# Last stage of a mixture-of-experts block: VectorE adds both partial sums of every group, and the weights are transposed and copied ahead

## The chip, the cores and the metric

The kernel runs on one core of a Trainium2 chip. The metric is the device time of one execution in microseconds (us). Engines are TensorE (PE), VectorE (DVE), ScalarE (ACT), GpSimd (POOL) and SyncE (SP), which issues most of the DMAs. They work side by side and wait for one another on semaphores.

## The reference

4096 tokens of 256 features pass through a gated recurrent layer and then a mixture-of-experts layer; each adds a layer-normed result to its input. What matters here is the end of the second one:

```python
    gate_up = jnp.einsum('th,ehd->etd', x, gate_up_proj) + gate_up_proj_bias[:, None, :]
    ...
    out = jnp.einsum('etd,edh->eth', (up + 1.0) * glu, down_proj) + down_proj_bias[:, None, :]
    out = out * router_scores.T[:, :, None]
    out = out.sum(axis=0)
    ...
x = x + _layernorm(_L0_ffn_ref(_layernorm(x, axis=-1), ...), axis=-1)
```

Each token has four experts with a score. So its output is the sum of four expert products, each times its score, plus the scores (16 of them, 12 zero) times the biases `down_proj_bias`, then layer-normed and added to the token's input.

## The kernel before

**The stages ahead.** A recurrent stage works on eight blocks of 512 tokens and routes every token's row to its experts' regions in HBM. Then 143 tiles of 128 routed rows go through their expert; GpSimd scatters each tile's result with an accumulating indirect DMA into one of two arrays in HBM, `sums0` and `sums1`, in turn (L1050). The two arrays together hold each token's expert sum.

**The last stage** adds it all up, in eight groups of 512 tokens (`NBLK` groups, `BT` = 4 rows of tokens per partition in each):

- SyncE waits for all scatters, then issues two loads a group, `sums0` into `z[g]` and `sums1` into `z2[g]` (L490, L491), of 512 KB each. Semaphores `blk_in[g]` and `z2_in[g]` tell when they have landed.
- TensorE transposes a group's weights `Wd` (`transpose_weights`, L728; four transposes into one of two PSUM banks, so group g waits for the copy of group g - 2), ScalarE copies them to `sT[g]` in SBUF (`evac_weights`, L965), and TensorE multiplies them with the biases (`biases`, L735; into one of three PSUM buffers, so group g waits until the total of group g - 3 has read its own).
- VectorE makes the total of a group (`total`, L1460): both sums, times a scale `y_inv`, plus the bias product. Groups 0 to 3 (`g < PAIRED`) take two adds on VectorE (L1466, L1468). For groups 4 to 7 GpSimd adds the two sums first (`both`, L1055, with the add at L1058), into `z2[g]`, and VectorE does one add (L1472).
- VectorE takes statistics of each total (L1482). Groups are normalised in three batches, `BATCHES = ((0, 1, 2, 3), (4, 5, 6), (7,))`: after a batch's last group VectorE aggregates (L1485), and computes the scale `r4` and shift `mr4` with a chain of ten small instructions (L1487, `newton` at L1077 to L1084, L1491). `rz_ready` says so.
- ScalarE normalises a group in place (`norm_z`, L982, instruction L987), four instructions a group, and for the last group only shifts the input rows (`shift_last`, L974, instruction L979), which VectorE then adds to the scaled total (`add_last`, L1500).
- GpSimd stores groups 0 to 6 with DMAs that add to the rows already in `out` (L1066); SyncE stores group 7 in two halves (L495).

The order on each engine is written out by hand. TensorE begins with the transposes of groups 0 and 1, and then has the bias of a group and the transposes of the group two further on in turn. ScalarE copies four groups' weights, then, for each of seven groups, copies the weights of the group four further on (while there are any) and normalises the group. GpSimd has its four adds ahead of all stores.

Of the kernel before, what the change touches and what calls it, by code (L numbers as in the profile page):

```python
# [27 lines left out]
NBLK = TOKENS // BLK  # L28
# [29 lines left out]
ROOT_A, ROOT_B = 0.375 * 0.703952253, 0.375 * 0.703952253 * 2.38924456  # L58
SUMS = 2
BATCHES = ((0, 1, 2, 3), (4, 5, 6), (7,))  # L60
PAIRED = 4
PART = 1024
PARTS_GU, PARTS_DN = E * KT * 2 * FF // PART, E * KT * DIM // PART
PARTS = PARTS_GU + PARTS_DN
# [67 lines left out]
def build(nc, x, w_in, w_gate, b_gate, rms_w, w_out, w_router, b_router, w_gu, b_gu, w_dn, b_dn,  # L132
# [3 lines left out]
    ALU = mybir.AluOpType  # L136
# [5 lines left out]
    with ctx:  # L142
# [3 lines left out]
        def sem(name):  # L146
            return ctx.enter_context(nc.semaphore(name))
# [143 lines left out]
        blk_in = [sem(f"blk_in{b}") for b in range(NBLK)]  # L291
# [30 lines left out]
        zero_ready, zero_sent, x1_sent = sem("zero_ready"), sem("zero_sent"), sem("x1_sent")  # L322
        sT_mm, sT_ready = sem("sT_mm"), sem("sT_ready")
        bias_mm, t_ready, rz_ready, yz_ready = sem("bias_mm"), sem("t_ready"), sem("rz_ready"), sem("yz_ready")
        out_sent, both_ready = sem("out_sent"), sem("both_ready")
        shift_ready, last_ready, last_sent = sem("shift_ready"), sem("last_ready"), sem("last_sent")

        block = ctx.enter_context(nc.Block())
# [173 lines left out]
        def _(pe):  # L502
# [225 lines left out]
            def transpose_weights(g):  # L728
                if g >= 2:
                    pe.wait_ge(sT_ready, g - 1)  # L730
                for u in range(BT):
                    last = nc.tensor.transpose(PS[0:E, 6 + g % 2, u * P:(u + 1) * P], Wd[:, BT * g + u, :], ident)
                last.then_inc(sT_mm, 1)
# [9 lines left out]

            pe.wait_ge(y2_ready, TILES + 2)
            pe.wait_ge(s_bdn, 16)
            transpose_weights(0)
            transpose_weights(1)
            for g in range(NBLK):
                biases(g)
                if g + 2 < NBLK:  # L750
                    transpose_weights(g + 2)


        @block.scalar
        def _(act):
# [209 lines left out]
            def evac_weights(g):  # L965
                act.wait_ge(sT_mm, g + 1)
                copy(sT[g], PS[0:E, 6 + g % 2, :]).then_inc(sT_ready, 1)
# [20 lines left out]
                                                bias=mr4[n][:, m + u:m + u + 1], scale=r4[n][:, m + u:m + u + 1])  # L988
                last.then_inc(yz_ready, 1)

            for g in range(4):
                evac_weights(g)
            for g in range(NBLK - 1):
                if g + 4 < NBLK:
                    evac_weights(g + 4)
                norm_z(g)
            shift_last(NBLK - 1)

# [1 line left out]
        @block.gpsimd  # L1000
        def _(pool):
            def wait(s, n):
                pool.wait_ge(s, n)
                if not isinstance(n, int):
                    pool.nop(nofuse=True)

            def scatter(t):

                b = t % 2
                per = BT * TOPK // 2  # L1010
                pool.wait_ge(slot_ready, t + 1)
                pool.wait_ge(lo_ready, t + 1)
                for jk in range(BT * TOPK if t < NBLK - 2 else AHEAD):
                    lane = jk % 2
                    if t or jk >= 2:
                        pool.wait_ge(rows_sent[lane], 16 * (per * t + jk // 2))
                    idx = slot[b][:, jk:jk + 1].bitcast(u32)
                    pool.indirect_dma_start(routed, bass.IndirectOffsetOnAxis(ap=idx, axis=0),  # L1018
                                            rows[b][:, jk // TOPK, :], None).then_inc(rows_sent[lane], 16)

            pool.wait_ge(nrow_out, 16)
            for e in range(E):
                if e % 2 == 0:
                    pool.wait_ge(s_moe[e // 2], 16)
                    pool.wait_ge(squared, 2 + PARTS_DN + e + 1)
                pool.dma_start(W[:, (GU0 + 1 + e) * PART:(GU0 + 2 + e) * PART].rearrange("p (k x) -> p k x", k=KT),  # L1026
                               neg_mem[e:e + 1, :].unsqueeze(1).to_broadcast([P, KT, 2 * FF]),
                               accum_op=ALU.add).then_inc(minus_done, 16)

            for t in range(NBLK - 1):  # L1030
                scatter(t)

            def late_row(n):
                t, jk = divmod(BT * TOPK * (NBLK - 2) + AHEAD + n, BT * TOPK)
                if jk == 0:
                    pool.wait_ge(slot_ready, t + 1)
                    pool.wait_ge(lo_ready, t + 1)
                idx = slot[t % 2][:, jk:jk + 1].bitcast(u32)
                pool.indirect_dma_start(routed, bass.IndirectOffsetOnAxis(ap=idx, axis=0),
                                        rows[t % 2][:, jk // TOPK, :], None).then_inc(rows_sent[jk % 2], 16)  # L1040

            for j in range(TILES):
                u = j % YU
                pool.wait_ge(meta_in[j % MU], 16 * (j // MU + 1))
                if j == 0:
                    pool.wait_ge(zero_sent, 16 * SUMS)
                pool.wait_ge(y2_ready, j + 3)
                if j >= SUMS:
                    pool.wait_ge(y_sent[(j - SUMS) % YU], 16 * ((j - SUMS) // YU + 1))
                pool.indirect_dma_start(sums[j % SUMS], bass.IndirectOffsetOnAxis(ap=dst[j % MU], axis=0),  # L1050
                                        yb[u], None, compute_op=ALU.add).then_inc(y_sent[u], 16)
                if j % 2 and j // 2 < 2 * BT * TOPK - AHEAD:
                    late_row(j // 2)

            def both(g):  # L1055
                pool.wait_ge(blk_in[g], 32)
                pool.wait_ge(z2_in[g], 16)
                nc.gpsimd.tensor_tensor(z2[g].rearrange("p u d -> p (u d)"), z[g].rearrange("p u d -> p (u d)"),  # L1058
                                        z2[g].rearrange("p u d -> p (u d)"), ALU.add).then_inc(both_ready, 1)

            for g in range(PAIRED, NBLK):
                both(g)
            pool.wait_ge(x1_sent, 16 * (NBLK - 1))
            for g in range(NBLK - 1):
                pool.wait_ge(yz_ready, g + 1)
                pool.dma_start(out_v[:, BT * g:BT * (g + 1), :], z[g], accum_op=ALU.add).then_inc(out_sent, 16)  # L1066
# [3 lines left out]
        def _(dve):  # L1070
# [389 lines left out]
            def total(g):  # L1460
                flat, flat2 = [a[g].rearrange("p u d -> p (u d)") for a in (z, z2)]
                bias = PS[:, 2 * (g % 3):2 * (g % 3) + 2, :].rearrange("p b x -> p (b x)")
                if g < PAIRED:
                    dve.wait_ge(blk_in[g], 32)
                    dve.wait_ge(bias_mm, g + 1)
                    L(v.scalar_tensor_tensor(flat, flat, y_inv, bias, ALU.mult, ALU.add))  # L1466
                    dve.wait_ge(z2_in[g], 16)
                    v.scalar_tensor_tensor(flat, flat2, y_inv, flat, ALU.mult, ALU.add).then_inc(t_ready, 1)  # L1468
                else:
                    dve.wait_ge(bias_mm, g + 1)  # L1470
                    dve.wait_ge(both_ready, g + 1 - PAIRED)
                    v.scalar_tensor_tensor(flat, flat2, y_inv, bias, ALU.mult, ALU.add).then_inc(t_ready, 1)  # L1472

            def batch(b):

# [74 lines left out]
```

## Time and profile before

| | |
|---|---|
| times of three runs | 746.56, 746.67, 748.28 us; median 746.67 |
| profiled execution | 747.17 us, of which 745.4 us are the span that the trace shows |
| busy over the span | PE 632.9, DVE 517.5, ACT 458.0, POOL 403.3 us |
| chain that ended last, by engine | PE 66%, DVE 10%, ACT 9%, DMA 8% |

The profile's busy times are sums over the whole span. The last stage, from about 682 us on, is 8% of it, and another set of engines works in it than in the stages ahead. So it is read from views of that stretch alone: the busy time by window, the waits, the chain of work that ended last, and the instructions in order of time. In those rows "W" is the SBUF array in which `z`, `z2` and `sT` lie, "small" holds the statistics and scales, "PS" is PSUM, "X" holds input rows. An idle time in brackets stands ahead of the first instruction of its row, with what ended it. "W<-W,small,PS 128x1024" is an instruction on 128 partitions of 1024 numbers each.

### The profile page before, as it was taken

How to read it: one execution, taken by the hardware profiler on the slowest of the kernel's cores; microseconds unless marked ns; L12 is line 12 of the kernel's file. 1: busy time of each engine (PE TensorE's matmuls, PEld its weight loads, DVE VectorE, ACT ScalarE, POOL GpSimd, SP SyncE). 2: the span in 40 equal slices, each digit the busy share in tenths (PEclk: the TensorE clock that was granted, in tenths of full speed). 3: DMA queues.
4: the chain of work that ended last, by engine and by line, in shares of the span. 5: the costliest groups of instructions: out<-in, count | busy, mean ns of one | idle time of the engine just before them, and what ended most of it. 6: DMA issues, size and time to landing. Idle time of an engine off the chain costs nothing.

```text
span 745.4 us, 13253 instructions
## 1 busy us (share of the span) xinstructions
PE 632.9 (85%) x3666; PEld 408.4 (55%) x3666; DVE 517.5 (69%) x1468; ACT 458.0 (61%) x929; POOL 403.3 (54%) x302
## 2 busy tenths in 40 slices
PE   6988979888998954598999999999999999985460
PEld 2454646555564643455666666666666666653240
DVE  3737687876788786877777777777777777751964
ACT  3689787546656525365776677677667766750054
POOL 0012213447677646546777887666666666663342
PEclk9999989796999965599999999999999999995555
DMA  7979999653233224256888877777776776646967
GB/s 234 419 304 156 275 237 293 185 171 124 88 117 121 99 90 139 95 102 111 188 170 164 131 132 118 113 114 115 116 114 106 117 108 101 100 57 144 342 99 127
DMA packets 110694, 114.32 MB, mean 153 GB/s; under 512 B 31426, under 2 KB 100306, under 8 KB 108962
## 3 DMA queue, kind: packets, MB, share of 16 engines
q0 software_dynamic: 34784, 49.70, 38.9%
q1 hardware_dynamic: 75842, 63.79, 28.7%
q8 instruction: 34, 0.56, 0.3%
q14 instruction: 34, 0.28, 0.1%
HBM read 54.94 MB, written 58.51 MB: 152 GB/s over the span
## 4 chain that ended last, share of the span: by engine, by line
PE 66%; DVE 10%; ACT 9%; DMA 8%; issue 3%; POOL 1%; SPq 0%; ACTq 0%; DVEq 0%; POOLq 0%
PE PS L683 8%; PE PS L684 8%; PE PS L685 8%; PE PS L531 7%; DMA routed<-arena,small 6%; PE PS L672 4%; PE PS L703 4%; PE PS L704 4%; PE PS L691 4%; PE PS L705 4%; PE PS L566 3%; PE PS L558 2%; DMA sums<-arena 1%; PE PS L541 1%; ACT arena L777 1%
## 5 line engine op out<-in xcount | busy, mean ns | idle before, releaser
L1050 POOL DMA_INDIRECT sums<-arena x143 | 223.2, 1561 | 107.5 <-ACT arena L757 42.9
L1018 POOL DMA_INDIRECT routed<-arena,small x104 | 117.7, 1132 | 77.7 <-DMA routed<-arena,small 52.7
L1446 DVE TENSOR_SCALAR arena<-PS,small 128x256 f32<-128x256 f32 x143 | 77.7, 543 | 90.0 <-ACT arena L960 89.9
L531 PE MATMUL PS<-arena 128*128 128x512 f32 x256 | 130.9, 656 | 7.5 <-ACT arena L757 7.4
L960 ACT ACTIVATE arena<-PS,small 128x256 f32<-128x256 f32 x143 | 67.7, 473 | 104.7 <-PE PS L685 104.7
L757 ACT ACTIVATE arena<-PS 128x512 f16<-128x512 f16 (+1 forms) x179 | 104.5, 590 | 26.5 <-PE PS L574 10.9
L683 PE MATMUL PS<-W,arena 128*128 x286 | 109.6, 383 | 0.2 <-DVE arena L1448 0.2
L684 PE MATMUL PS<-W,arena 128*128 x286 | 109.5, 383 | 0.0
L685 PE MATMUL PS<-W,arena 128*128 x286 | 109.5, 383 | 0.0
L531 PEld LDWEIGHTS PS<-arena 128*128 128x128 f32 x256 | 51.7, 213 | 64.7 <-issue 60.8
L703 PE MATMUL PS<-W,arena 128*128 x286 | 78.1, 273 | 4.8 <-DVE arena L1436 4.7
L704 PE MATMUL PS<-W,arena 128*128 x286 | 78.1, 273 | 0.0
L705 PE MATMUL PS<-W,arena 128*128 x286 | 78.0, 273 | 0.0
L777 ACT ACTIVATE arena<-PS,small 128x512 f32<-128x512 f32 x64 | 43.7, 692 | 52.0 <-PE PS L531 51.9
L1026 POOL DMA_DIRECT2D W<-neg_mem x16 | 19.8, 1485 | 102.5 <-DMA neg_mem<-arena 53.0
L1448 DVE SCALAR_TENSOR_TENSOR arena<-arena,small 128x256 f32<-128x256 f32 x143 | 69.4, 485 | 5.1
L757 ACT ACTIVATE arena<-PS,arena 128x256 f32<-128x256 f32 x143 | 69.0, 482 | 6.3 <-PE PS L705 6.1
L1436 DVE SCALAR_TENSOR_TENSOR arena<-PS,small,arena 128x256 f16<-128x256 f32 x143 | 68.2, 478 | 1.8 <-ACT arena L757 1.7
L757 ACT ACTIVATE arena<-PS,small 128x256 f16<-128x256 f32 x143 | 68.0, 475 | 0.0
L672 PEld LDWEIGHTS PS<-ident,arena 128*128 128x128 f16 x572 | 43.5, 99 | 36.9 <-issue 6.8
L1447 DVE SCALAR_TENSOR_TENSOR arena<-arena,PS 128x256 f32<-128x256 f32 x143 | 58.6, 410 | 0.0
L672 PE MATMUL PS<-ident,arena 128*128 128x128 f16 x572 | 56.0, 221 | 1.1 <-ACT arena L757 0.8
(185 smaller groups left out, 1039.3 us busy)
## 6 DMA issues: line engine op xcount, KB each, us to landing
arena<-routed SPq DMA_DIRECT2D x143, 128.0 KB, 2.5
W<-w_gu SPq DMA_DIRECT2D x8, 1024.0 KB, 23.9
W<-neg_mem POOLq DMA_DIRECT2D x16, 512.0 KB, 10.8
sums<-zero SPq DMA_DIRECT2D x2, 4096.0 KB, 34.3
W<-sums SPq DMA_DIRECT2D x16, 512.0 KB, 9.0
X<-x SPq DMA_DIRECT2D x8, 512.0 KB, 5.7
W<-w_dn SPq DMA_DIRECT2D x4, 1024.0 KB, 11.2
out<-X SPq DMA_DIRECT2D x7, 512.0 KB, 3.1
```

The source lines that it names most:

```text
L531: last = mm(PS[:, 2 + c % 2, :], WcT[:, k, c * P:(c + 1) * P], xT[:, k, :], start=(k == 0), stop=(k == KT - 1))
L672: last = nc.tensor.transpose(xT16[:, k * P:(k + 1) * P], xrow[j % UN][:, k * P:(k + 1) * P], ident16[:, :])
L683: mm(acc, xq[j % NX][:, k, :], hi, start=(k == 0), stop=False)
L684: mm(acc, xq[j % NX][:, k, :], lo, start=False, stop=False)
L685: last = mm(acc, xq[j % NX][:, KT + k, :], hi, start=False, stop=(k == KT - 1))
L703: mm(acc, ah[j % 2][:, k, :], hi, start=(k == 0), stop=False)
L704: mm(acc, ah[j % 2][:, k, :], lo, start=False, stop=False)
L705: last = mm(acc, al[j % 2][:, k, :], hi, start=False, stop=(k == KT - 1))
L757: return nc.scalar.activation(o, i, ACT.Copy, **kw)
L1018: pool.indirect_dma_start(routed, bass.IndirectOffsetOnAxis(ap=idx, axis=0), rows[b][:, jk // TOPK, :], None).then_inc(rows_sent[lane], 16)
L1050: pool.indirect_dma_start(sums[j % SUMS], bass.IndirectOffsetOnAxis(ap=dst[j % MU], axis=0), yb[u], None, compute_op=ALU.add).then_inc(y_s ...
L1446: L.send(v.tensor_scalar(up[j % 2], acc[:, FF:2 * FF], gu_hi, gu_lo, ALU.min, ALU.max))
```

## The change

VectorE does both adds for all eight groups; `both` and its semaphore are gone, and GpSimd has only the stores. TensorE transposes all eight groups' weights and then does the eight biases. ScalarE copies the weights of all eight groups before it normalises any.

```diff
--- before.py
+++ after.py
@@ -58,7 +58,6 @@
 ROOT_A, ROOT_B = 0.375 * 0.703952253, 0.375 * 0.703952253 * 2.38924456
 SUMS = 2
 BATCHES = ((0, 1, 2, 3), (4, 5, 6), (7,))
-PAIRED = 4
 PART = 1024
 PARTS_GU, PARTS_DN = E * KT * 2 * FF // PART, E * KT * DIM // PART
 PARTS = PARTS_GU + PARTS_DN
@@ -322,7 +321,7 @@
         zero_ready, zero_sent, x1_sent = sem("zero_ready"), sem("zero_sent"), sem("x1_sent")
         sT_mm, sT_ready = sem("sT_mm"), sem("sT_ready")
         bias_mm, t_ready, rz_ready, yz_ready = sem("bias_mm"), sem("t_ready"), sem("rz_ready"), sem("yz_ready")
-        out_sent, both_ready = sem("out_sent"), sem("both_ready")
+        out_sent = sem("out_sent")
         shift_ready, last_ready, last_sent = sem("shift_ready"), sem("last_ready"), sem("last_sent")
 
         block = ctx.enter_context(nc.Block())
@@ -743,12 +742,10 @@
 
             pe.wait_ge(y2_ready, TILES + 2)
             pe.wait_ge(s_bdn, 16)
-            transpose_weights(0)
-            transpose_weights(1)
+            for g in range(NBLK):
+                transpose_weights(g)
             for g in range(NBLK):
                 biases(g)
-                if g + 2 < NBLK:
-                    transpose_weights(g + 2)
 
 
         @block.scalar
@@ -988,11 +985,9 @@
                                                 bias=mr4[n][:, m + u:m + u + 1], scale=r4[n][:, m + u:m + u + 1])
                 last.then_inc(yz_ready, 1)
 
-            for g in range(4):
+            for g in range(NBLK):
                 evac_weights(g)
             for g in range(NBLK - 1):
-                if g + 4 < NBLK:
-                    evac_weights(g + 4)
                 norm_z(g)
             shift_last(NBLK - 1)
 
@@ -1052,14 +1047,6 @@
                 if j % 2 and j // 2 < 2 * BT * TOPK - AHEAD:
                     late_row(j // 2)
 
-            def both(g):
-                pool.wait_ge(blk_in[g], 32)
-                pool.wait_ge(z2_in[g], 16)
-                nc.gpsimd.tensor_tensor(z2[g].rearrange("p u d -> p (u d)"), z[g].rearrange("p u d -> p (u d)"),
-                                        z2[g].rearrange("p u d -> p (u d)"), ALU.add).then_inc(both_ready, 1)
-
-            for g in range(PAIRED, NBLK):
-                both(g)
             pool.wait_ge(x1_sent, 16 * (NBLK - 1))
             for g in range(NBLK - 1):
                 pool.wait_ge(yz_ready, g + 1)
@@ -1460,16 +1447,11 @@
             def total(g):
                 flat, flat2 = [a[g].rearrange("p u d -> p (u d)") for a in (z, z2)]
                 bias = PS[:, 2 * (g % 3):2 * (g % 3) + 2, :].rearrange("p b x -> p (b x)")
-                if g < PAIRED:
-                    dve.wait_ge(blk_in[g], 32)
-                    dve.wait_ge(bias_mm, g + 1)
-                    L(v.scalar_tensor_tensor(flat, flat, y_inv, bias, ALU.mult, ALU.add))
-                    dve.wait_ge(z2_in[g], 16)
-                    v.scalar_tensor_tensor(flat, flat2, y_inv, flat, ALU.mult, ALU.add).then_inc(t_ready, 1)
-                else:
-                    dve.wait_ge(bias_mm, g + 1)
-                    dve.wait_ge(both_ready, g + 1 - PAIRED)
-                    v.scalar_tensor_tensor(flat, flat2, y_inv, bias, ALU.mult, ALU.add).then_inc(t_ready, 1)
+                dve.wait_ge(blk_in[g], 32)
+                dve.wait_ge(bias_mm, g + 1)
+                L(v.scalar_tensor_tensor(flat, flat, y_inv, bias, ALU.mult, ALU.add))
+                dve.wait_ge(z2_in[g], 16)
+                v.scalar_tensor_tensor(flat, flat2, y_inv, flat, ALU.mult, ALU.add).then_inc(t_ready, 1)
 
             def batch(b):
```

TensorE's instructions at the end of the program, from the last expert product on; L732 and L731 are the transposes (`transpose_weights`), L740 and L739 the bias products. Before:

```order
L705 MATMUL PS<-W,arena 128x256
L732 MATMUL PS<-K,Wd 16x128 x8
L740 MATMUL PS<-Bdn,W 128x256 x4
L732 MATMUL PS<-K,Wd 16x128 x4
L740 MATMUL PS<-Bdn,W 128x256 x4
L732 MATMUL PS<-K,Wd 16x128 x4
L740 MATMUL PS<-Bdn,W 128x256 x4
L732 MATMUL PS<-K,Wd 16x128 x4
L740 MATMUL PS<-Bdn,W 128x256 x4
L732 MATMUL PS<-K,Wd 16x128 x4
L740 MATMUL PS<-Bdn,W 128x256 x4
L732 MATMUL PS<-K,Wd 16x128 x4
```

Now:

```order
L702 ISA
L702 MATMUL PS<-W,arena 128x256
L703 ISA
L703 MATMUL PS<-W,arena 128x256
L704 MATMUL PS<-W,arena 128x256
L731 MATMUL PS<-K,Wd 16x128 x32
L739 MATMUL PS<-Bdn,W 128x256 x32
```

The transposes of six groups have moved ahead of the first bias product.

ScalarE's instructions at its end; those that write "W" from PSUM are the copies of weights, and L987 and L984 the normalisations. Before:

```order
L757 ACTIVATE arena<-PS,small 128x256
L757 ACTIVATE arena<-PS,arena 128x256 x2
L757 ACTIVATE W<-PS 16x512 x5
L987 ACTIVATE W<-W,small 128x256 x4
L757 ACTIVATE W<-PS 16x512
L987 ACTIVATE W<-W,small 128x256 x4
L757 ACTIVATE W<-PS 16x512
L987 ACTIVATE W<-W,small 128x256 x4
L757 ACTIVATE W<-PS 16x512
L987 ACTIVATE W<-W,small 128x256 x16
L979 ACTIVATE X<-X,small 128x256 x4
```

Now:

```order
L754 ACTIVATE arena<-PS,small 128x256
L754 ACTIVATE arena<-PS,arena 128x256 x2
L754 ACTIVATE W<-PS 16x512 x8
L984 ACTIVATE W<-W,small 128x256 x28
L976 ACTIVATE X<-X,small 128x256 x4
```

The three copies that stood between and behind normalisations have moved ahead of the first one.

VectorE's instructions from the end of batch 0's scale to the statistics of group 6; L1472, L1452 and L1454 are adds, L1482 and L1464 the statistics. Before:

```order
L1491 SCALAR_TENSOR_TENSOR small<-small 128x16
L1472 SCALAR_TENSOR_TENSOR W<-W,small,PS 128x1024
L1482 BN_STATS small<-W 128x6 x4
L1472 SCALAR_TENSOR_TENSOR W<-W,small,PS 128x1024
L1482 BN_STATS small<-W 128x6 x4
L1472 SCALAR_TENSOR_TENSOR W<-W,small,PS 128x1024
L1482 BN_STATS small<-W 128x6 x4
L1485 BN_AGGR small<-small 128x2 x12
```

Now:

```order
L1473 SCALAR_TENSOR_TENSOR small<-small 128x16
L1452 SCALAR_TENSOR_TENSOR W<-W,small,PS 128x1024
L1454 SCALAR_TENSOR_TENSOR W<-W,small 128x1024
L1464 BN_STATS small<-W 128x6 x4
L1452 SCALAR_TENSOR_TENSOR W<-W,small,PS 128x1024
L1454 SCALAR_TENSOR_TENSOR W<-W,small 128x1024
L1464 BN_STATS small<-W 128x6 x4
L1452 SCALAR_TENSOR_TENSOR W<-W,small,PS 128x1024
L1454 SCALAR_TENSOR_TENSOR W<-W,small 128x1024
L1464 BN_STATS small<-W 128x6 x4
L1467 BN_AGGR small<-small 128x2 x12
```

Each of these groups has a second add between the first and the statistics.

## Rows read from the trace of the kernel before

**Rows 1.** Windows: busy us (instructions) by engine, granted clock, DMA share, GB/s.
```profile
680.00:690.00 10.00, 1.38 (x5) 0.87 (x4) 3.71 (x6) 0.59 (x1) 0.00 (x0) 0.50 0.78 234
...
720.00:725.00 5.00, 5.00 (x13) 3.92 (x12) 3.03 (x7) 1.57 (x4) 1.45 (x2) 0.50 1.22 191
```

**Rows 2.** Waits from 680 us on: who waited for whom, total us, times, longest.
```profile
ACT W L987 <- DVE small L1491: 37.6, 2, 30.7
...
PE PS L740 <- ACT W L757: 15.9, 1, 15.9
...
DVE W L1472 <- PE PS L740: 5.8, 2, 3.8
```

**Rows 3.** Chain that ended last, in order of time: start, us, what.
```profile
711.65 2.07 ACT W L987 x4
713.73 0.48 ACT W L757
```

**Rows 4.** Timeline, GpSimd's adds and VectorE: start, us, engine, line, shapes, [idle before].
```profile
703.36 2.34 POOL L1058 TENSOR_TENSOR W<-W 128x1024 f32<-128x1024 f32 x1 [0.51 <-DMA W<-sums]
703.55 2.19 DVE L1077 TENSOR_SCALAR small<-small 128x16 int32<-128x16 int32 x1
...
706.37 2.34 POOL L1058 TENSOR_TENSOR W<-W 128x1024 f32<-128x1024 f32 x1 [0.67 <-DMA W<-sums]
706.41 2.33 DVE L1081 TENSOR_TENSOR small<-small 128x16 f32<-128x16 f32 x1
...
709.22 2.36 POOL L1058 TENSOR_TENSOR W<-W 128x1024 f32<-128x1024 f32 x1 [0.51 <-DMA W<-sums]
709.42 2.20 DVE L1491 SCALAR_TENSOR_TENSOR small<-small 128x16 f32<-128x16 f32 x1
```

**Rows 5.** Timeline, VectorE in batch 0: first and second adds, aggregation.
```profile
686.01 1.28 DVE L1466 SCALAR_TENSOR_TENSOR W<-W,small,PS 128x1024 f32<-128x1024 f32 x1 [18.90 <-DMA W<-sums]
...
694.12 1.27 DVE L1466 SCALAR_TENSOR_TENSOR W<-W,small,PS 128x1024 f32<-128x1024 f32 x1
...
695.42 1.28 DVE L1468 SCALAR_TENSOR_TENSOR W<-W,small 128x1024 f32<-128x1024 f32 x1
...
698.06 1.26 DVE L1466 SCALAR_TENSOR_TENSOR W<-W,small,PS 128x1024 f32<-128x1024 f32 x1
...
702.12 1.18 DVE L1485 BATCH_NORM_AGGREGATE small<-small 128x2 f32<-128x6 f32 x16
```

**Rows 6.** Timeline, batches 1 and 2: VectorE, ScalarE and the last three stores.
```profile
725.48 0.91 DVE L1485 BATCH_NORM_AGGREGATE small<-small 128x2 f32<-128x6 f32 x12
...
728.50 6.00 ACT L987 ACTIVATE W<-W,small 128x256 f32<-128x256 f32 x12 [6.93 <-DVE small L1491]
...
730.96 1.28 POOL L1066 DMA_DIRECT2D out<-W  x1 [7.36 <-ACT W L987]
731.14 0.38 DVE L1485 BATCH_NORM_AGGREGATE small<-small 128x2 f32<-128x6 f32 x4
...
733.37 0.17 DVE L1491 SCALAR_TENSOR_TENSOR small<-small 128x4 f32<-128x4 f32 x1
733.87 2.59 POOL L1066 DMA_DIRECT2D out<-W  x2 [1.63 <-issue]
734.41 1.69 ACT L979 ACTIVATE X<-X,small 128x256 f32<-128x256 f32 x4
```

**Rows 7.** Windows of the stores: columns as in the first group.
```profile
714.00:731.50 17.50, 11.85 (x28) 8.01 (x28) 11.23 (x42) 10.16 (x22) 5.77 (x5) 0.50 0.82 120
731.50:745.40 13.90, 0.00 (x0) 0.00 (x0) 3.37 (x15) 4.60 (x11) 3.33 (x3) 0.50 0.91 151
```

**Rows 8.** Timeline, TensorE's transposes and biases.
```profile
668.85 1.04 PE L732 MATMUL PS<-K,Wd 128*16 128x128 f32 x8 [0.65 <-ACT arena L757]
...
674.66 1.02 PE L732 MATMUL PS<-K,Wd 128*16 128x128 f32 x4
...
693.60 3.78 PE L740 MATMUL PS<-Bdn,W 16*128 16x256 f32 x8
```


## What the change will do to the time

> **What bounds the kernel now.** I read the stages first, then the waits of the last one, then its chain, and last the instructions on it.
> The windows tell where the last stage stands: by 680 us TensorE has next to nothing left to do (1.38 us busy in ten) and runs at a granted clock of 0.50, its 1.2 GHz level, while DMA loads the sums [rows 1]. Nothing the diff touches is on the path before that: VectorE's first add starts at 686.01, and what ends its 18.90 us of idleness is a load [rows 5]. So the question is the stretch from 686.01 to 745.4, the span's end, 59.4 us.
> The waits of that stretch show three engines waiting in a ring [rows 2]: ScalarE for the last VectorE instruction of a batch (L1491; 37.6 us in two waits, the longest 30.7), TensorE for a ScalarE copy of weights (L757; 15.9), VectorE for TensorE's bias product (L740; 5.8 in two waits). The chain in order of time shows the ring turning: ScalarE normalises group 0 (711.65), then copies weights (713.73), and what follows is TensorE's bias of group 5, for which VectorE waits [rows 2, 3]. The copy is late only because the order of ScalarE's queue puts it behind the normalisation of group 0, which waits for batch 0's scale; TensorE needs no more than the copy.
> The third thing is seen by setting GpSimd's adds beside VectorE's small instructions [rows 4]. Three VectorE instructions on 128x16 take 2.19, 2.33 and 2.20 us. Each begins 0.04 to 0.20 us after a GpSimd add of 2.34 to 2.36 us has begun, and ends within 0.05 us of that add's end (705.70 and 705.74, 708.71 and 708.74, 711.58 and 711.62). The same kind of work on four columns takes 0.17 us when GpSimd adds nothing, 733.37 [rows 6]. VectorE is held while GpSimd adds, three times, on the chain.
>
> **The change, part by part.**
> *GpSimd's four adds go.* What they cost on the path is the three holds: about 2.19 + 2.33 + 2.20, less 0.18 of real work each (a sixteen-column instruction is little more than the 0.17 of four) = 6.2 us. The add of group 4 lies beside statistics instructions and costs nothing there (aggregation of sixteen rows from 702.12, 1.18 us, is 74 ns each; twelve rows take 0.91, 76 ns each) [rows 5, 6]. Batch 0's scale is then done at 711.62 - 6.2 = 705.4 instead of 711.6, and ScalarE's first normalisation starts at 705.45.
> *VectorE gets a second add for groups 4 to 7.* Groups 0 to 3 already have both adds; one such group takes 3.94 us from its first add to the next group's (694.12 to 698.06), the second add 1.28 of it [rows 5]. Four more are 5.1 us of VectorE, all on the path: 3.9 in batch 1 and 1.3 in batch 2. What does this wait for? The loads: GpSimd's add of group 5, 6 and 7 started when its loads were in, at 703.36, 706.37 and 709.22 [rows 4]; VectorE comes to these groups at 709.3, 713.2 and 720.3. They are in.
> *ScalarE copies all eight weights first, TensorE transposes all eight first.* The instructions are the same in number; only the order moves. What it removes is VectorE's 5.8 us of waiting for the bias of groups 5 and 6 [rows 2]: bias 5 needs only its weights and the total of group 2, which is done before that of group 3 begins at 698.06 [rows 5]. What it may cost is at the front: bias 0 now stands behind six more groups of transposes. The first two groups of transposes start at 668.85; a group of four takes 1.02 us once the clock is low, and a group's bias 3.78 (its row counts eight matmuls, two for each of four products) [rows 8]. Eight groups of transposes are 8.2 us, and with a ScalarE copy of 0.48 [rows 3] between one pair and the next they end by 679 to 680; biases 0, 1 and 2 then end by 684, 688 and 692. VectorE wants them at 686.01 and, at 3.94 a group, 690 and 694.1 [rows 5]. So it is hidden by the loads, with about 2 us of cover at the slowest; at the higher clock, which TensorE still has as it enters (the first two groups take 1.04 together) [rows 8], by more. If that cover were gone, each us too late would move the whole stage by one us.
> *The stores.* GpSimd's seven accumulating stores are issued 6 to 8 us earlier, and VectorE is now busy beside them. A row of the windows gives their price: with the DMA engines full (share 1.22) [rows 1], four stores use 0.82 x 17.5 / 1.22 = 11.8 us, 2.9 each; and the last three with the plain store of group 7 use 0.91 x 13.9 / 1.22 = 10.4 us [rows 7]. The first four would start about 710, when the loads are through, and be through at about 722; the next is issued near 722.8. They do not meet, and even if all seven ran in a row they would be done by 710 + 11.8 + 10.4 = 732, before the 735 that the sum gives. No cost.
>
> **The sum.** Batch 0 done 705.4. Groups 4, 5, 6: 705.35 + 3 x 3.94 = 717.2, and the last group of a batch reaches aggregation 0.1 later (698.06 to 702.12 is 4.06) [rows 5]: 717.3. From there to ScalarE's start is 3.02, as before (725.48 to 728.50) [rows 6]: 720.3. Before, it was 728.5: 8.2 us earlier (6.2 from the holds, 5.8 from the waits, less 3.9 for adds). Batch 2: two adds and statistics, 4.06 from 720.2, then 2.4 (731.14 to 733.54) [rows 6]: 726.7, against 733.54, 6.9 earlier. ScalarE ends its twelve normalisations at 720.3 + 6.0 = 726.3 and so waits 0.4 us for batch 2; it starts its last four at 726.7 instead of 734.41, 7.7 earlier.
> The tail after that is DMA: from 731.5 the engines are mostly idle and the DMA share is 0.91 to the end [rows 7]. Its bulk hangs on the stores of groups 4 to 6, which move by 8.2; the last store by 7.7. I take 8.0, between the two. Span 745.4 - 8.0 = 737.4. The profiled execution took 747.17, 1.77 more than its span, so 739.2; it lies 0.5 above the median of 746.67, and against that median the forecast is **738.7 us**, 1.1% less.
>
> **A rule that speaks against it.** First the rows: GpSimd's issue of the fifth store takes 1.28 us beside small VectorE instructions, and the last two together 2.59, 1.30 each, though VectorE's last adds (L1500, two inputs in SBUF) follow ScalarE's shift of 734.41 in that stretch [rows 6]. No hold is seen. The Trainium skill (SBUF — State Buffer, "Who interferes with whom" and the warning in "SBUF: two separate sides") says that GpSimd writes the descriptors of its DMAs through a port pair shared with VectorE, and that a VectorE instruction in a two-port mode locks it out until it ends; two-input instructions, it infers, do not. VectorE is to be busy beside all seven stores now, so a wider reading of that rule is rival (a); by the rows the sum stays as it is.
>
> **The rivals.**
> (a) *The stores are held by VectorE's adds.* Bounds: nothing (the usual 1.28), or one whole add of 1.28 us for the issue that opens the tail. For: in the kernel before, VectorE waited 5.8 us of the stretch in which the first four were issued [rows 2], so adds seldom stood beside an issue. Against: the 1.30 beside L1500 [rows 6], and the last adds ahead of 722.8 end by then. It gives 738.7 + 1.3 = 740.0; with the same once more, behind it, 741.3.
> (b) *The holds do not go*, because something other than GpSimd's adds made them, the loads for instance, which run in that stretch. Then batch 0 is done at 711.62 as before, groups 4 to 6 end at 723.5, ScalarE starts at 726.5, 2.0 earlier: 744.7, which this kernel's measurement cannot tell from no change. Against: the ends agree three times within 0.05 us, and the loads had run for 20 us without such a hold.
> (c) *Slower: the accumulating stores become the bound.* They now start against a VectorE that is never idle, and if that starved GpSimd's descriptors, their 2.9 us would rise. Seven of them and 0.5 of one for the plain store lie between 710 and some 2 us before the end; the point from which the kernel is slower is (743.6 - 710) / 7.5 = 4.5 us each, and at 5 us the time is 746.7 + 7.5 x 0.5 = 750.4. Against: nothing in the trace shows a store at that price.
> (d) *Below the forecast.* GpSimd issues its sixth store at 733.87, 0.9 us after the 733.0 at which a fifth and a normalisation of 2.0 more would allow it [rows 6]; if that lateness is not repeated, the tail may be up to 1 us shorter: 737.7.
>
> **How the numbers follow.** The forecast, with (d), 0.79; (a) 0.10; (b) and anything else that eats nearly all 0.08; (c) 0.03. Range: 736.8 (1 us from (d), and another for the spread of runs) to 742.0 (past the end of (a)); it leaves out (b), (c) and some 0.04 below. What this kernel's measurement can tell from no change is about 0.3%, 2.2 us. Faster by more 0.89, within 0.08, slower 0.03.
>
> **What would show it.** In the changed kernel: no VectorE instruction of 128x16 over 0.2 us after 703; ScalarE's first normalisation near 705.5, its fifth near 720.3; no wait of VectorE for a bias product; the second add of groups 4 to 7 at 1.28 us; eight weight copies before 680; stores of 1.3 us to issue, and the DMA share falling near 735. It is wrong if VectorE still stalls without GpSimd, if the first add starts after 686.0 because of a bias, or if the DMA tail from the fifth store's issue is longer than 14.4 us (730.96 to the end) [rows 6].

## The result

The changed kernel takes 744.05 us (median of 20 runs, 735.48 to 751.39). The kernel before, run beside it and counted with the three runs shown, takes 750.52 (median of 20, 746.56 to 757.23). The ratio is 0.990 with a 95% interval of 0.987 to 0.993: about 1.0% faster. (The ratio leaves out three of the changed kernel's 20 runs as slow, more than 1.5% above its fastest; the two medians alone give 0.991.) The forecast was 1.1% faster, but from a level of 746.67; so 744.05 lies outside the range of 736.8 to 742.0.

The profiled execution took 745.80 us with a span of 744.0, hardly less than the 745.4 before. Set against VectorE's first add, the picture is another. The waits from 678 us on (who waited for whom; total us, times, longest):

```profile
ACT W L984 <- DVE small L1473: 43.0, 2, 36.1
...
DVE W L1452 <- DMA W<-sums: 23.8, 1, 23.8
...
PE PS L739 <- DVE W L1454: 17.0, 5, 12.7
```

TensorE no longer waits for ScalarE, nor VectorE for TensorE: of [rows 2] only the first kind is left, ScalarE waiting for a batch's scale. The timeline of the last stage (start, us, engine, line, shapes, idle before):

```profile
670.92 1.04 PE L731 MATMUL PS<-K,Wd 128*16 128x128 f32 x8 [0.65 <-ACT arena L754]
...
674.76 1.08 PE L731 MATMUL PS<-K,Wd 128*16 128x128 f32 x8 [0.20 <-ACT W L754]
...
675.77 7.44 PE L739 MATMUL PS<-Bdn,W 16*128 16x256 f32 x24
...
692.95 1.28 DVE L1452 SCALAR_TENSOR_TENSOR W<-W,small,PS 128x1024 f32<-128x1024 f32 x1 [23.76 <-DMA W<-sums]
...
709.24 1.18 DVE L1467 BATCH_NORM_AGGREGATE small<-small 128x2 f32<-128x6 f32 x16
...
710.67 0.17 DVE L1064 TENSOR_SCALAR small<-small 128x16 int32<-128x16 int32 x1
...
712.36 0.18 DVE L1473 SCALAR_TENSOR_TENSOR small<-small 128x16 f32<-128x16 f32 x1
...
712.57 7.97 ACT L984 ACTIVATE W<-W,small 128x256 f32<-128x256 f32 x16 [36.10 <-DVE small L1473]
713.76 1.28 DVE L1454 SCALAR_TENSOR_TENSOR W<-W,small 128x1024 f32<-128x1024 f32 x1
...
716.41 1.26 DVE L1452 SCALAR_TENSOR_TENSOR W<-W,small,PS 128x1024 f32<-128x1024 f32 x1
...
724.41 0.91 DVE L1467 BATCH_NORM_AGGREGATE small<-small 128x2 f32<-128x6 f32 x12
```

```profile
727.43 6.00 ACT L984 ACTIVATE W<-W,small 128x256 f32<-128x256 f32 x12 [6.89 <-DVE small L1473]
...
729.89 1.28 POOL L1053 DMA_DIRECT2D out<-W  x1 [7.31 <-ACT W L984]
...
732.80 2.60 POOL L1053 DMA_DIRECT2D out<-W  x2 [1.63 <-issue]
...
733.81 1.71 ACT L976 ACTIVATE X<-X,small 128x256 f32<-128x256 f32 x4 [0.38 <-DVE small L1473]
```

L1064 and L1473, the instructions that took 2.19 and 2.20 us in [rows 4], take 0.17 and 0.18. A group with both adds still takes 3.96 us (712.45 to 716.41). But the first add starts at 692.95, 6.9 us later than in [rows 5]. Measured from the first add, the steps of the sum and the two profiles are:

| us after VectorE's first add | before | forecast | after |
|---|---|---|---|
| first normalisation | 25.6 | 19.4 | 19.6 |
| fifth normalisation | 42.5 | 34.3 | 34.5 |
| shift of group 7 | 48.4 | 40.7 | 40.9 |
| end of the span | 59.4 | 51.4 | 51.05 |

The last stage is 8.3 us shorter, and every step of it within 0.35 us of the forecast. What moved against it lies ahead. ScalarE's last copy of a tile's result (L757 before, L754 after), GpSimd's last scatter and SyncE's first load show it; before, then after:

```profile
668.32 0.47 ACT L757 ACTIVATE arena<-PS,arena 128x256 f32<-128x256 f32 x1 [1.22 <-PE PS L705]
...
678.36 1.56 POOL L1050 DMA_INDIRECT sums<-arena  x1 [0.95 <-DMA sums<-arena]
...
682.29 0.39 SPq L490 DMA_DIRECT2D W<-sums  x1
```

```profile
670.39 0.47 ACT L754 ACTIVATE arena<-PS,arena 128x256 f32<-128x256 f32 x1 [1.22 <-PE PS L704]
...
685.22 1.56 POOL L1045 DMA_INDIRECT sums<-arena  x1 [0.94 <-DMA sums<-arena]
689.24 0.39 SPq L489 DMA_DIRECT2D W<-sums  x1
```

The copy is 2.1 us later; after it GpSimd still issues seven scatters instead of five, some 2.2 us each, and the first load follows 18.9 us behind the copy instead of 14.0. The diff does not reach this part of the program. The runs had to tell whether the change did it all the same.

### The profile page after: what moved, and what is told of

Its sections match the earlier page's. It is cut to its first block, busy times and chain, and to the rows that moved or that the text cites. A ratio compares the mean times of both kernels' runs of the same rounds, so it can differ in the third digit from the quotient of the medians.

```text
span 744.0 us, 13251 instructions
## 1 busy us (share of the span) xinstructions
PE 630.7 (85%) x3666; PEld 408.0 (55%) x3666; DVE 517.2 (70%) x1472; ACT 459.0 (62%) x929; POOL 392.8 (53%) x298
## 4 chain that ended last, share of the span: by engine, by line
PE 66%; DVE 11%; DMA 10%; ACT 7%; issue 4%; POOL 1%; SPq 0%; DVEq 0%; ACTq 0%; POOLq 0%
PE PS L682 8%; PE PS L683 8%; PE PS L684 8%; PE PS L530 8%; DMA routed<-arena,small 6%; PE PS L671 4%; PE PS L690 4%; PE PS L702 4%; PE PS L703 4%; PE PS L704 4%; PE PS L565 3%; DMA sums<-arena 3%; PE PS L557 2%; PE PS L540 2%; PE PS L573 1%
## 5 line engine op out<-in xcount | busy, mean ns | idle before, releaser
L754 ACT ACTIVATE arena<-PS 128x512 f16<-128x512 f16 (+1 forms) x179 | 104.5, 590 | 27.3 <-PE PS L573 11.3
L530 PEld LDWEIGHTS PS<-arena 128*128 128x128 f32 x256 | 51.8, 213 | 65.1 <-issue 61.5
L754 ACT ACTIVATE arena<-PS,arena 128x256 f32<-128x256 f32 x143 | 69.2, 484 | 6.2 <-PE PS L704 6.0
L754 ACT ACTIVATE arena<-PS,small 128x256 f16<-128x256 f32 x143 | 68.1, 476 | 0.0
```

The lines of the kernel that those rows point to most:

```text
L530: last = mm(PS[:, 2 + c % 2, :], WcT[:, k, c * P:(c + 1) * P], xT[:, k, :], start=(k == 0), stop=(k == KT - 1))
L754: return nc.scalar.activation(o, i, ACT.Copy, **kw)
```

## The experiments

"Last stage" is the time from VectorE's first add to the end of the span, "tail" the time from ScalarE's last copy of a tile's result to the first load. All kernels in one table (one run of before at 1293.6 us is left out); what follows takes them one by one. First load, tail and last stage come from one profiled run each, and the experiments ran in four sets on four chips, so small differences of medians between rows can be those of chips: the kernel before, in the same sets, had medians of 750.8, 748.9 and 748.4, and one run of 757.6 in the fourth.

| kernel | first load | tail | last stage | median (runs) |
|---|---|---|---|---|
| before, four profiles | 682.3, 688.2, 685.2, 685.3 | 14.0, 16.0, 15.9, 18.1 | 59.4, 59.3, 59.3, 59.6 | 750.4 (91, all sets) |
| after, two profiles | 689.2, 684.6 | 18.9, 20.6 | 51.05, 51.1 | 744.0 (30) |
| adds only | 686.4 | 19.5 | 54.4 | 745.2 (10) |
| order only | 685.4 | 17.1 | 51.8 | 745.6 (10) |
| after, with idle adds on GpSimd | 689.8 | 24.2 | 55.3 | 750.6 (1) |
| adds between scale and stores | 687.1 | 19.4 | 47.9 | 741.5 (12) |
| before, plain scatters, two profiles | 671.9, 667.7 | 5.0, 5.3 | 59.8, 60.0 | 738.5 (4), 736.8 (6) |
| after, plain scatters | 672.1 | 4.6 | 51.0 | 729.4 (6) |
| adds between, plain scatters | 674.5 | 4.8 | 48.4 | 727.5 (6) |

**Both kernels again, unchanged.**

> The changed kernel a second time, unchanged, to see what of its time repeats. My theory: the last stage, from VectorE's first add to the end of the span, repeats (51.0 us, within 0.4), and what differs between executions lies ahead of it, in how many of GpSimd's scatters are still to go when the last tile's product is done (7 in the profile of the changed kernel, 5 in that of before, some 2.3 us each). Rival 1: the change itself lengthens the scatters' tail; then the first add again comes 22 us after TensorE's first weight transpose, against 17.2 before. Rival 2: the last stage itself varies by several us.

> The kernel before a second time, unchanged, beside the others. My theory: its last stage repeats at 59.4 us within 0.4, and the stretch from TensorE's first weight transpose to VectorE's first add does not (17.2 us the first time; anything between 15 and 24). Rival 1 (the change lengthens the scatters' tail): 17 again. Its time against itself should be 1.00 within 0.5%.

Measured: the changed kernel 742.74 us (median of 10; ratio 0.993, 0.989 to 0.996), the kernel before 752.61 (ratio to itself 1.002, 0.998 to 1.007). The last stage repeats: 51.1 and 59.3. The tail does not: 20.6 and 16.0. Rival 2, a last stage that varies, falls by this; rival 1 does not, since both tails of the kernel before are shorter than both of the changed one. It is taken up at the end.

**One half of the change: the adds.**

> VectorE does both adds of all groups and GpSimd none, but the order of the transposes and weight copies is that of before. If GpSimd's adds made the holds: no small instruction on 128x16 above 0.2 us, ScalarE's first normalisation 3.3 us after the aggregation starts (9.5 before). The copy of group 5's weights still stands behind the normalisation of group 0, so VectorE waits some 2.6 us for the bias of group 5 and 0.7 for that of group 6: ScalarE's fifth normalisation 4.8 us earlier than before against the first add, last stage 54.6 us, time 0.6% less. If the loads made the holds: 9.5 us again, and with the added adds a last stage of 59 to 64 us, time equal or up to 0.6% more.

Against the changed kernel the edit is:

```diff
-            for g in range(NBLK):
-                transpose_weights(g)
+            transpose_weights(0)
+            transpose_weights(1)
             for g in range(NBLK):
                 biases(g)
+                if g + 2 < NBLK:
+                    transpose_weights(g + 2)
...
-            for g in range(NBLK):
+            for g in range(4):
                 evac_weights(g)
             for g in range(NBLK - 1):
+                if g + 4 < NBLK:
+                    evac_weights(g + 4)
                 norm_z(g)
```

Measured: last stage 54.4 us, 5.0 less than before (forecast 4.8); 745.17 us, ratio 0.993 (0.989 to 0.997). The timeline shows the wait that the old order leaves:

```profile
711.48 0.57 ACT L756 ACTIVATE W<-PS 16x512 f32<-16x512 f32 x1
...
712.11 3.78 PE L739 MATMUL PS<-Bdn,W 16*128 16x256 f32 x8 [9.79 <-ACT W L756]
...
715.99 1.28 DVE L1456 SCALAR_TENSOR_TENSOR W<-W,small,PS 128x1024 f32<-128x1024 f32 x1 [2.57 <-PE PS L739]
...
716.76 7.19 PE L739 MATMUL PS<-Bdn,W 16*128 16x256 f32 x16
...
720.65 1.28 DVE L1456 SCALAR_TENSOR_TENSOR W<-W,small,PS 128x1024 f32<-128x1024 f32 x1 [0.62 <-PE PS L739]
```

ScalarE's copy for group 5 (711.48) stands behind the normalisation of group 0, TensorE's bias starts at 712.11, and VectorE's add of group 5 waits 2.57 us for it, that of group 6 another 0.62.

**The other half: the order.**

> Transposes and weight copies of all eight groups first, but GpSimd still adds the sums of groups 4 to 7. If GpSimd's adds made the holds, they are still there: three small instructions of 2.2 us, ScalarE's first normalisation 9.5 us after the aggregation starts. VectorE then needs 2.7 us for each of groups 4 to 6 without a wait for a bias: the fifth normalisation 5.7 us earlier than before against the first add, last stage 53.7 us, time 0.8% less. If the order is worth nothing by itself (the wait for the bias only moves elsewhere), the last stage is 59.4 us.

Against the kernel before the edit is:

```diff
-            transpose_weights(0)
-            transpose_weights(1)
             for g in range(NBLK):
+                transpose_weights(g)
+            for g in range(NBLK):
                 biases(g)
-                if g + 2 < NBLK:
-                    transpose_weights(g + 2)
...
-            for g in range(4):
+            for g in range(NBLK):
                 evac_weights(g)
             for g in range(NBLK - 1):
-                if g + 4 < NBLK:
-                    evac_weights(g + 4)
                 norm_z(g)
```

Measured: last stage 51.8 us, 7.6 less than before and 1.9 better than expected; 745.63 us, ratio 0.997 (0.992 to 1.001), so the time alone does not tell it from no change. The timeline of the scale of batch 0 tells why the last stage is shorter than expected:

```profile
706.50 2.33 POOL L1054 TENSOR_TENSOR W<-W 128x1024 f32<-128x1024 f32 x1 [0.67 <-DMA W<-sums]
706.67 2.20 DVE L1074 TENSOR_TENSOR small<-small 128x16 f32<-128x16 f32 x1
...
709.51 2.34 POOL L1054 TENSOR_TENSOR W<-W 128x1024 f32<-128x1024 f32 x1 [0.68 <-DMA W<-sums]
709.54 2.35 DVE L1078 SCALAR_TENSOR_TENSOR small<-small 128x16 f32<-128x16 f32 x1
...
712.34 0.18 DVE L1487 SCALAR_TENSOR_TENSOR small<-small 128x16 f32<-128x16 f32 x1
712.35 2.39 POOL L1054 TENSOR_TENSOR W<-W 128x1024 f32<-128x1024 f32 x1 [0.50 <-DMA W<-sums]
712.43 1.28 DVE L1468 SCALAR_TENSOR_TENSOR W<-W,small,PS 128x1024 f32<-128x1024 f32 x1
712.55 7.97 ACT L985 ACTIVATE W<-W,small 128x256 f32<-128x256 f32 x16 [38.23 <-DVE small L1487]
...
715.07 1.26 DVE L1468 SCALAR_TENSOR_TENSOR W<-W,small,PS 128x1024 f32<-128x1024 f32 x1
```

There are two holds, not three. The chain's last small instruction (712.34) began 0.01 us ahead of GpSimd's last add (712.35), and then took 0.18 us. So the price of the adds, once the order is mended, hangs on which engine starts first: 0.7 us of last stage here, and by estimate 2.0 more when the third add comes first (2.20 instead of 0.18, as in [rows 4]). No run of this order had that third hold; all four profiles of the kernel before have three. VectorE's add that follows (712.43), with one input in SBUF and one in PSUM, runs beside that GpSimd add at its usual 1.28 us, and so do the statistics behind it: the next add starts at 715.07, 2.64 later.

**The holds by themselves.**

> The changed kernel, and GpSimd once more adds 128x1024 four times as the loads of groups 4 to 7 land, now numbers that nobody reads, in memory of its own. If GpSimd's adds hold VectorE: two or three of the small instructions on 128x16 take 2.0 to 2.4 us instead of 0.18, the stretch from batch 0's aggregation to ScalarE's first normalisation grows from 3.3 to 7.5 or 9.5 us, and the last stage from 51.1 to 55.2 or 57.3 us, though nothing waits for these adds. If the holds came from the loads or from the data that both engines share: 3.3 us and 51.1 us as in the changed kernel.

```diff
+            spare = [arena[:, 9120 + n * PART:9120 + (n + 1) * PART] for n in range(5)]
+            for g in range(4, NBLK):
+                pool.wait_ge(blk_in[g], 32)
+                pool.wait_ge(z2_in[g], 16)
+                nc.gpsimd.tensor_tensor(spare[g - 3], spare[0], spare[0], ALU.add)
```

```profile
710.80 1.91 POOL L1054 TENSOR_TENSOR arena<-arena 128x1024 f32<-128x1024 f32 x1 [0.95 <-DMA W<-sums]
711.00 1.75 DVE L1069 TENSOR_SCALAR small<-small 128x16 int32<-128x16 int32 x1
...
713.82 1.89 POOL L1054 TENSOR_TENSOR arena<-arena 128x1024 f32<-128x1024 f32 x1 [1.11 <-DMA W<-sums]
713.84 1.91 DVE L1075 SCALAR_TENSOR_TENSOR small<-small 128x16 f32<-128x16 f32 x1
...
716.67 1.89 POOL L1054 TENSOR_TENSOR arena<-arena 128x1024 f32<-128x1024 f32 x1 [0.96 <-DMA W<-sums]
717.40 2.25 DVE L1459 SCALAR_TENSOR_TENSOR W<-W,small 128x1024 f32<-128x1024 f32 x1
```

Nobody waits for these adds and nobody shares their data, yet VectorE is held: L1069 takes 1.75 instead of 0.17, L1075 1.91 instead of 0.18, and the second add of group 4 (L1459, both inputs in SBUF) 2.25 instead of 1.28. That is 1.58 + 1.73 + 0.97 = 4.3 us, and the last stage is 55.3, 4.3 longer than the changed kernel's. The stretch from the aggregation to the first normalisation is 6.6 us, short of the 7.5 expected for two holds: these adds are shorter, and the third one fell on the second add of group 4. The cause of the holds is GpSimd's add itself, not the loads.

**A version meant to beat both.**

> A version meant to beat both: the order of the changed kernel, but GpSimd adds the sums of group 4 as they land, beside statistics, and of groups 5 and 6 only after batch 0's scale is ready, one ahead of the first store and one behind it; VectorE does both adds of groups 0 to 3 and 7. If GpSimd's adds hold only VectorE instructions with two inputs in SBUF and those of the scale's chain, no instruction is held, groups 4 to 6 need 2.7 us each instead of 3.94, ScalarE's fifth normalisation comes 31.8 us after VectorE's first add (34.5 in the changed kernel), last stage 48.4 us, time 0.3 to 0.4% below the changed kernel and 1.4% below before. If an add on GpSimd also holds statistics or VectorE's one-add totals, up to 4.7 us are lost: 51 to 53 us.

```diff
-PAIRED = 4
+PAIRED = (4, 5, 6)
...
-            for g in range(PAIRED, NBLK):
-                both(g)
+            both(4)
             pool.wait_ge(x1_sent, 16 * (NBLK - 1))
+            pool.wait_ge(rz_ready, 1)
+            both(5)
             for g in range(NBLK - 1):
+                if g == 1:
+                    both(6)
                 pool.wait_ge(yz_ready, g + 1)
```

(The diff is against the kernel with the new order alone; the two tests of `PAIRED` in `total`, which follow it, are left out here.)

```profile
710.08 1.28 DVE L1471 SCALAR_TENSOR_TENSOR W<-W,small,PS 128x1024 f32<-128x1024 f32 x1
...
710.30 2.35 POOL L1054 TENSOR_TENSOR W<-W 128x1024 f32<-128x1024 f32 x1 [2.71 <-DVE small L1490]
711.39 1.41 DVE L1481 BATCH_NORM_STATS2 small<-W 128x6 f32<-128x256 f32 x4
712.60 1.38 POOL L1065 DMA_DIRECT2D out<-W  x1
712.77 1.28 DVE L1471 SCALAR_TENSOR_TENSOR W<-W,small,PS 128x1024 f32<-128x1024 f32 x1
713.45 2.91 POOL L1054 TENSOR_TENSOR W<-W 128x1024 f32<-128x1024 f32 x1
...
716.46 1.28 DVE L1471 SCALAR_TENSOR_TENSOR W<-W,small,PS 128x1024 f32<-128x1024 f32 x1 [0.97 <-POOL W L1054]
...
722.25 6.00 ACT L985 ACTIVATE W<-W,small 128x256 f32<-128x256 f32 x12 [4.07 <-DVE small L1490]
```

GpSimd's adds (710.30 and 713.45) lie beside one-add totals and statistics, and none of these is held; VectorE waits 0.97 us for the second of them, whose row of 2.91 us begins while GpSimd still issues the store of 712.60. Last stage 47.9 us, 3.1 below the changed kernel (expected 48.4). The time, 741.51 us (ratio to before 0.991, 0.987 to 0.995), cannot tell it from the changed kernel's 742.74 and 744.05: against the medians of the kernel before in the same sets the gains are 7.4, 8.1 and 6.5 us.

**What moves the level.**

> The kernel before, but GpSimd's scatters of the tiles' results overwrite the rows in HBM instead of adding to them (so the sums hold one addend each); everything behind them is the same. If the scatters' tail is what moves the start of the last stage from run to run: a plain scatter lands sooner than the 3.9 us of an accumulating one, no more than three are left when the last tile's result is copied, the first load is issued 6 to 9 us after that copy (14.0 to 20.6 in the six profiles so far), the last stage still takes 59.3 us, and the ten runs lie within 6 us of one another (8 to 17 for the kernel before). If the level comes from the stages ahead: as wide a spread as before, around a median some 9 us lower.

```diff
                 pool.indirect_dma_start(sums[j % SUMS], bass.IndirectOffsetOnAxis(ap=dst[j % MU], axis=0),
-                                        yb[u], None, compute_op=ALU.add).then_inc(y_sent[u], 16)
+                                        yb[u], None).then_inc(y_sent[u], 16)
```

Measured: 738.52 us, four runs within 3.2. The tail is 5.0 us (6 to 9 were expected), the last stage 59.8. The copy and the first load in the second such profile:

```profile
662.43 0.47 ACT L757 ACTIVATE arena<-PS,arena 128x256 f32<-128x256 f32 x1 [1.22 <-PE PS L705]
```

```profile
667.70 0.39 SPq L490 DMA_DIRECT2D W<-sums  x1
```

From the one to the other are 5.3 us. With that part of the spread out of the way, the three kernels were timed again:

> Once more the kernel before with scatters that overwrite instead of adding (the sums then hold one addend each), as the base of the next two. If the accumulating scatters make the spread, all its runs lie within 6 us, median 738.5 within 1.

> The changed kernel with scatters that overwrite instead of adding (the sums hold one addend each). With the spread of the scatters' tail out of the way the times should show what the last stage shows: 59.4 - 51.1 = 8.3 us less than the kernel before with the same scatters, 730.2 us within 1. If part of the gain is given back ahead of the last stage, as the pair of medians 750.5 and 744.1 (6.5 us) could be read: 6.5 us less, 732.0.

> The version with GpSimd's adds between the scale and the stores, with scatters that overwrite instead of adding (the sums hold one addend each). By its last stage of 47.9 us it should be 3.1 us below the changed kernel with the same scatters, 11.4 below the kernel before with them: 727.1 us within 1. If the times of 741.5 and 742.7 with the accumulating scatters tell its worth, it is 1.2 below the changed kernel.

Measured, six runs each: 736.77 (733.02 to 740.48), 729.37 (727.12 to 733.06), 727.47 (723.58 to 731.65). The 6 us that I expected for the kernel before was missed with 7.5, and so was 738.5 within 1. Nor do these times show that the spread fell much: the 18 us of the kernel before (742.7 to 760.7) are those of 91 runs, and ten of its runs in one set lay within 8.2 too. What the scatters add is seen in the profiles. From the first of the 143 scatters to the last it is 344.8 to 347.0 us in the four with plain scatters, and 352.6 to 361.9 in the ten with accumulating ones; the first scatter starts anywhere from 319.6 to 329.6. So the level has two sources, the stages ahead of the scatters and the accumulating scatters themselves. They partly cancel (an early start tends to go with a long stretch), so that the first loads range over 7.5 us with accumulating scatters and over 6.8 with plain ones. The change is worth 7.4 us here, and the version with adds between 1.9 more, between the two readings in both cases; with six runs each, and a spread of 6 to 8 us in each six, neither pair of readings is told apart, and the 1.9 is not clear of noise.

**Whether the change lengthens the tail.**

> The kernel before a third time. So far the stretch from ScalarE's last copy of a tile's result to the first load of sums was 14.0 and 16.0 us in the two profiles of the kernel before, and 17.1 to 24.2 in the six of kernels with all or part of the change. If that is chance, this and the next lie anywhere from 14 to 24, and at least one above 17; if the change lengthens the scatters' tail, both lie below 17. The last stage is 59.3 us.

> The kernel before a fourth time, for the same question: chance, 14 to 24 us from the last copy to the first load and at least one of the two above 17; the change's doing, both below 17. The last stage is 59.3 us.

Measured: 15.9 and 18.1. By the rule set beforehand that is chance, one above 17. It is a thin verdict: the four profiles of the kernel before average 16.0, the six with all or part of the change 19.9, and their first loads 685.2 and 687.1. A late copy tends to go with a short tail (672.15 with 16.0, 664.0 with 20.6), so the first load is the fairer measure, and 1.9 us is less than its range of 7.5. Over all runs the medians differ by 6.4 us (91 against 30), the last stages by 8.3. The other kernels with the new order fall short in the same way against the kernel before in their sets, 5.2 us for 7.6 (order only) and 7.4 for 11.4 (adds between), and the one with the old order does not, 5.6 for 5.0 (adds only); but two medians of the kernel before in one set differ by 1.8 as well (750.8 and 752.6). Whether some 1 to 2 us are given back ahead of the last stage, or whether that is spread, stays open; no part of the diff was found that could do it.

## Why the prediction was right and wrong

**Right: what bounds the last stage.** Three engines waiting in a ring, and GpSimd's adds on top. Each half of the change, undone alone, brings back the wait or the hold that it was to remove (2.57 and 0.62 us of waiting; two holds of 2.20 and 2.35), and GpSimd's adds alone bring back holds. So rival (b) fell.

**Right: the adds of VectorE and the sum.** 3.94 us a group was forecast, and 3.94 and 3.96 measured; first normalisation, fifth, shift and end came 0.2, 0.2, 0.2 and -0.35 us from the forecast.

**Right in sign, too large in size: the cover at the front.** The transposes of eight groups, with the copies between them, took 4.9 us (670.92 to 675.84), not 11: TensorE came from the expert products, and its granted clock was 1.00 in that stretch, the 2.4 GHz level, at which a group took 0.54 us. Biases 0 to 2 had all ended at 683.2, 12.3 us after the first transposes; the forecast gave them 23. That is 9.7 us before VectorE's first add, not 2 for the first of them alone; 4.9 of it come from the loads, since the first add followed the first transposes by 22.0 us here and by 17.2 before.

**Right: the stores.** Issues take 1.27 to 1.37 us beside VectorE's adds, the last two 2.60 together. Rival (a) did not occur, and neither did (d): the sixth store is late again ("issue", 1.63 us), as in [rows 6]. From the fifth store's issue to the end are 14.1 us (14.4 before), so rival (c) did not occur either.

**Not additive.** The sum took the holds at 6.2 us and the waits at 5.8 as separate terms, less 3.9 for the adds. They are separate in that sum, but not each by itself: the adds alone gained 5.0, the order alone 7.6, both 8.3. Without the bias waits, GpSimd's adds save VectorE 3.9 us of adds in batch 1, about what two holds (2.02 + 2.17) cost it there.

**Wrong: the last line of the sum, the level.** The mechanism of the last stage held; the step that failed is the base that its gain was taken from. The line "against that median the forecast is 738.7 us" took three runs of 746.56 to 748.28 for the kernel's time, and the range gave "another [1 us] for the spread of runs". 91 runs of the same kernel have a median of 750.4, and only 11 of them lie at or below 746.7. Beside the changed kernel it took 750.52: of the 5.4 us between 744.05 and 738.7, 3.9 are this base, and 1.5 a gain of 6.5 us instead of 8.0, whose cause stays open. That the three runs shown were so low, and so close together, was chance as far as the runs show. The profile shown was such an execution too: its first load at 682.3 is the earliest of the ten with accumulating scatters (up to 689.8). The row that said so was there: VectorE idle for 18.90 us ahead of its first add [rows 5], ended by a load. I read "what ends its 18.90 us of idleness is a load" as the end of the matter and did not ask what the loads wait for. They wait for GpSimd's queue of scatters, which is not tied to TensorE's end: after the last copy 5 to 10 scatters were still to be issued in the ten profiles, and the first load came 14.0 to 24.2 us behind it. Had I priced it with a spread of 7 us for the first load, the range would have held 744.05. The gain itself, 0.9 to 1.0% for 1.1%, was not what failed.

## What to carry to other kernels

Time a stage from its own first instruction, and ask what the wait ahead of it hangs on before taking the level for given: a queue that runs nearly as slowly as the loop that feeds it (here 2.2 us a scatter in the tail, and 2.4 us a tile, by the spacing of the plain scatters) ended anywhere from 678.4 to 685.9 us in the ten profiles. When two engines hold one another, look for the place where the same work runs beside instructions that are not held; moving GpSimd's adds there shortened the last stage by 3.1 us more than giving them all to VectorE, though the times could not tell the two apart. A copy that stands behind an unrelated wait in an engine's queue is a wait for everyone downstream of it; here its removal alone took 7.6 us off the last stage, some 2 of them because one hold happened not to occur.

## What the runs showed of the hardware

- A GpSimd add of 128x1024 held VectorE's small two-input instructions and TENSOR_SCALAR (2.19 to 2.35 us instead of 0.17 or 0.18), and an add of 1.9 us held one with both inputs in SBUF (2.25 instead of 1.28), the small ones to within 0.05 us of its own end; it did not hold statistics (1.41 for four), aggregation, or an add with one input in PSUM (1.28). A small instruction that began 0.01 us ahead of the add took its usual 0.18 us.
- The Trainium skill (SBUF — State Buffer, "Who interferes with whom") says that a VectorE instruction with two inputs in SBUF and a GpSimd instruction that reads SBUF exclude one another for a whole instruction, that one in a two-port mode and GpSimd do so too, and that one with at most one input in SBUF, outside those modes, does not meet GpSimd. The runs agree where VectorE was held (2.19 to 2.35 us), down to the add with one input in PSUM (1.28); whether the held TENSOR_SCALAR ran in a two-port mode, they do not show. It also infers that the two-input tensor_tensor does not hold GpSimd's issue of a DMA. The trace agrees for these adds: the store issues beside them took 1.27 to 1.37 us.
- A GpSimd add of two tensors of 128x1024 took some 2.34 us (2.33 to 2.49), and some 1.9 with the same tensor as both inputs (1.89 to 2.06).
- Taking the accumulation out of the scatters shortened their issue on GpSimd from 1.54 to 0.96 us (medians), the tail from 14 to 24 us to 5, and the time of the kernel before by 10 to 12 us.
